# A Mamba, MLP and attention block on one Trainium2 core: v made behind q and k, the first transposed scores ahead of the last score unit, the attention's residual rows ahead of its last division

## The reference, cut to what matters

```
x1 = _ln(x) * (scale1 + 1.0) + shift1
qkv = (x1 @ mat_qkv_w.T + qkv_bias).reshape(B, L, 3, H, hd)      # qkv_bias: q_bias, zeros, v_bias
q, k, v = [jnp.transpose(qkv[:, :, i], (0, 2, 1, 3)) for i in range(3)]
q = _l2norm(q) * sm                                              # 16 heads of 16 channels
k = _l2norm(k)
probs = jax.nn.softmax(jnp.einsum('bhqd,bhkd->bhqk', q, k), axis=-1)
o = jnp.einsum('bhqk,bhkd->bhqd', probs, v)
attn_out = o @ proj_w.T + proj_b
x = x + attn_out * gamma1
...                                                              # a second layer norm and an MLP of width 1024
```

## Time and profile before

| | |
|---|---|
| median of 3 runs | 3436.22 us (3434.76 to 3437.71) |
| the profiled execution | 3437.39 us |
| its span | 3435.6 us, 60533 instructions |
| PE busy | 3272.0 us (95%) |
| DVE busy | 2798.0 us (81%) |
| ACT busy | 2803.2 us (82%) |
| POOL busy | 2501.9 us (73%) |
| TensorE's granted clock over the span | 0.977 of full speed |

### The profile page before, as it was taken

One profiled execution on the slowest core, in us unless ns is written; L12 is line 12 of the kernel. 1 busy time (PEld: TensorE's weight loads), 2 busy tenths in 40 slices (PEclk: granted clock), 3 DMA queues, 4 the chain that ended last, 5 costly groups with the idle time before them and its releaser, 6 DMA issues. The chain is left out here.

```text
span 3435.6 us, 60533 instructions
## 1 busy us (share of the span) xinstructions
PE 3272.0 (95%) x23720; PEld 2705.5 (79%) x23720; DVE 2798.0 (81%) x3009; ACT 2803.2 (82%) x4960; POOL 2501.9 (73%) x1104
## 2 busy tenths in 40 slices
PE   7999999999899999999989999999999999999998
PEld 6889898974488988897368898899637898888744
DVE  2899999976299999996639999999554999999761
ACT  1989999964498999995559999999356999999734
POOL 1899999960098999994029999999204999999700
PEclk9999999998999999999999999999989999999989
DMA  3221211100111121220021222212002221111000
GB/s 131 84 64 56 72 56 64 62 32 13 53 62 64 62 69 52 70 68 25 1 70 57 64 70 64 63 58 68 13 1 78 68 64 68 55 57 56 31 13 7
DMA packets 57088, 187.71 MB, mean 55 GB/s; under 512 B 6626, under 2 KB 12770, under 8 KB 55906
## 3 DMA queue, kind: packets, MB, share of 16 engines
q1 hardware_dynamic: 56802, 183.84, 16.0%
HBM read 180.65 MB, written 3.16 MB: 54 GB/s over the span
## 5 line engine op out<-in xcount | busy, mean ns | idle before, releaser
L543 POOL TENSOR_TENSOR states<-states,c_rows 128x1024 f32<-128x1024 f32 x1020 | 2394.7, 2382 | 499.0 <-DMA c_rows<-c_spill 411.8
L1356 DVE TENSOR_TENSOR_SCAN states<-decay,bank 128x512 f32<-128x512 f32 x2048 | 2350.9, 1203 | 214.8 <-ACT decay L684 143.0
L684 ACT ACTIVATE decay<-dt,a_log 128x512 f32<-128x512 f32 x2048 | 1307.2, 712 | 0.5 <-DVE states L1356 0.5
L937 PE MATMUL bank<-ident,states 128*128 128x128 f32 x8192 | 1237.3, 274 | 18.2 <-POOL states L543 0.3
L926 PE MATMUL bank<-ident,inflow_tok 128*128 128x128 f32 x6144 | 1046.3, 279 | 59.8 <-DVE states L1356 42.9
L678 ACT ACTIVATE inflow_tok<-dtx_tok,b_tok 128x512 f32<-128x512 f32 x1536 | 995.4, 714 | 61.8 <-PE bank L927 58.5
L937 PEld LDWEIGHTS bank<-ident,states 128*128 128x128 f32 x8192 | 955.0, 142 | 50.4 <-POOL states L543 47.9
L926 PEld LDWEIGHTS bank<-ident,inflow_tok 128*128 128x128 f32 x6144 | 707.5, 141 | 241.6 <-issue 128.9
L927 PE MATMUL bank<-b_diag,dtx_tok 128*128 128x128 f32 x4096 | 794.5, 276 | 0.0
L927 PEld LDWEIGHTS bank<-b_diag,dtx_tok 128*128 128x128 f32 x4096 | 621.0, 192 | 0.0
L1444 DVE TENSOR_REDUCE decay<-bank 128x1 f32<-128x512 f32 x256 | 159.7, 684 | 68.0 <-PE bank L1118 67.7
(11 more groups left out here) (152 smaller groups left out, 2039.3 us busy)
## 6 DMA issues: line engine op xcount, KB each, us to landing
c_rows<-c_spill SPq DMA_DIRECT2D x256, 512.0 KB, 3.7
xproj_w<-in_xproj_w SPq DMA_DIRECT2D x32, 320.0 KB, 4.3
in_w<-in_in_w SPq DMA_DIRECT2D x16, 512.0 KB, 4.9
in_w<-in_fc_w SPq DMA_DIRECT2D x8, 512.0 KB, 5.3
xproj_w<-in_w SPq DMA_DIRECT2D x8, 512.0 KB, 5.2
xproj_w<-in_fc_w SPq DMA_DIRECT2D x4, 1024.0 KB, 4.8
y_gated<-in_mod_w SPq DMA_DIRECT2D x1, 2048.0 KB, 7.4
x_ahead<-in_x SPq DMA_DIRECT2D x4, 512.0 KB, 5.6
```

The costliest lines, as they stand in the source:

```text
L543: pool.tensor_tensor(pair, pair, c_row, ALU.mult).then_inc(weighed, 1)
L684: act.activation(decay[:, r % SLOTS * KI + k, :], dt[:, d, k, :], ACT.Exp, scale=a_neg[:, d, k, s:s + 1]).then_inc(decay_ready, 1)
L937: last = pe.matmul(banks[KI + t][:, k * P:(k + 1) * P], states[:, r % SLOTS * KI + k, t * P:(t + 1) * P], ident[:], is_transpose=True, sta ...
L1356: dve.tensor_tensor_scan(states[:, slot, time], decay[:, slot, time], banks[k % INFLOW_BANKS][:, time], 0.0, ALU.mult, ALU.add).then_inc(s ...
```

## The change

It does four things.

- v is made after all four tiles of q and k, in banks 2 and 3 (two tiles to a bank). Its bias is put in the bank by a matmul with one row, ahead of the two of the product, and ACT (instead of DVE) copies it to `v_ones`, two tiles at a time. The five `WARM` matmuls are gone. The wait for v moves from in front of the first score unit to the third and the fourth, whose banks it uses.
- The ring of score banks starts at bank 1 instead of bank 0, and the ring of transposed scores at bank 6 instead of bank 3. So of the score units 31, 32 and 33, the first two wait for lead units 25 and 26 and the third for lead unit 30; before it was 30, 25 and 26.
- In period 0 the third score unit stands behind the four transposed scores.
- Three of the four pairs of `add_rows` for the attention's residual stand ahead of the last transpose of sums (one) and ahead of the last division's result (two); the fourth stands behind the transposes of o.

```diff
-WARM = 5
+V_BANK = 2
...
         def score_bank(u):
-            return banks[u % LEAD_BANKS] if u < LEAD else banks[score_slot(u) % S_BANKS]
+            return banks[u % LEAD_BANKS] if u < LEAD else banks[ring_bank(score_slot(u))]
+
+        def ring_bank(slot):
+
+            return (slot + 1) % S_BANKS
 
         def turn_bank(p):
-            return banks[turn_slot(p) % S_BANKS]
+            return banks[ring_bank(turn_slot(p))]
+
+        def t_bank(v):
+
+            return S_BANKS + (v + T_BANKS - 1) % T_BANKS
...
                 root(TT - 1)
+                act.wait_ge(ones_ready, b + 1)
+                for i in range(2):
+                    act.wait_ge(v_mm, b * TT + 2 * i + 2)
+                    act.activation(v_ones[:, 2 * i:2 * i + 2, :, 0:HD],
+                                   banks[V_BANK + i].rearrange("p (t h e) -> p t h e", t=2, e=HD), ACT.Copy).then_inc(v_ready, 1)
...
-                    act.activation(probs_t[v % len(probs_t)], banks[S_BANKS + v % T_BANKS], ACT.Exp,
+                    act.activation(probs_t[v % len(probs_t)], banks[t_bank(v)], ACT.Exp,
...
                     for kc in range(KD):
-                        pe.matmul(banks[QK_BANK + t % 2], h_t[:, kc, t * P:(t + 1) * P], qkv_w[:, kc, 0:2 * D],
-                                  start=(kc == 0), stop=(kc == KD - 1))
-                    for kc in range(KD):
-                        last = pe.matmul(banks[t][:, 0:D], h_t[:, kc, t * P:(t + 1) * P], qkv_w[:, kc, 2 * D:3 * D], start=(kc == 0), stop=(kc == KD - 1))
-                    last.then_inc(qkv_mm, 1)
+                        last = pe.matmul(banks[QK_BANK + t % 2], h_t[:, kc, t * P:(t + 1) * P], qkv_w[:, kc, 0:2 * D],
+                                         start=(kc == 0), stop=(kc == KD - 1))
+                    last.then_inc(qk_mm, 1)
                     if t == 0:
                         ln_turn(b, 2, 2)
                         ln_turn(b, 2, 3)
-                for w in range(WARM):
-                    pe.matmul(banks[TURN_BANK + 1], ident[:], qkv_w[:, w % KD, 0:2 * D], start=True, stop=True)
+
+                def value_tile(t):
+
+                    to = banks[V_BANK + t // 2][:, t % 2 * D:(t % 2 + 1) * D]
+                    pe.matmul(to, ident[0:1, 0:1].to_broadcast([1, P]), row_b[0:1, V_BIAS, :], start=True, stop=False,
+                              skip_group_check=True)
+                    for kc in range(KD):
+                        last = pe.matmul(to, h_t[:, kc, t * P:(t + 1) * P], qkv_w[:, kc, 2 * D:3 * D], start=False,
+                                         stop=(kc == KD - 1), skip_group_check=True)
+                    last.then_inc(v_mm, 1)
+
+                for t in range(TT):
+                    value_tile(t)
 
...
                 turn_heads(0)
-                pe.wait_ge(v_ready, (b + 1) * TT)
                 pe.wait_ge(q_t_first, b + 1)
...
                     if x < S_BANKS:
-                        pe.wait_ge(neg_ready, b * UNITS + lead_last(x) + 1)
+                        pe.wait_ge(neg_ready, b * UNITS + lead_last(ring_bank(x)) + 1)
...
                     elif u >= LEAD_BANKS:
                         pe.wait_ge(neg_ready, b * UNITS + u - LEAD_BANKS + 1)
+                    elif u in (V_BANK, V_BANK + 1):
+                        pe.wait_ge(v_ready, b * TT // 2 + u - V_BANK + 1)
...
-                    if v < LEAD_BANKS - S_BANKS:
-                        pe.wait_ge(neg_ready, b * UNITS + lead_last(S_BANKS + v) + 1)
+                    if v == 0:
+                        pe.wait_ge(qk_t_ready, (b + 1) * (2 * NG - 1))
                     elif v < T_BANKS:
-                        pe.wait_ge(qk_t_ready, (b + 1) * (2 * NG - 1))
+                        pe.wait_ge(neg_ready, b * UNITS + lead_last(t_bank(v)) + 1)
                     else:
                         pe.wait_ge(probs_t_ready, b * UNITS + v - T_BANKS + 1)
                     a = slice(i * LANE, (i + 1) * LANE)
-                    pe.matmul(banks[S_BANKS + v % T_BANKS], k_t[a, g, kt * P:(kt + 1) * P], q_t[a, g, :], start=True,
+                    pe.matmul(banks[t_bank(v)], k_t[a, g, kt * P:(kt + 1) * P], q_t[a, g, :], start=True,
                               stop=True).then_inc(scores_t_mm, 1)
...
                         scores_t(v)
                         scores(u + 1)
                         scores_t(v + 1)
-                        scores(u + 2)
+                        if j:
+                            scores(u + 2)
                     else:
                         scores_t(v)
                         scores_t(v + 1)
                     scores_t(v + 2)
                     scores_t(v + 3)
+                    if j == 0:
+                        scores(u + 2)
                     if j:
                         weigh(j - 1)
                     if j in TURN_PERIODS:
...
                 weigh(PERIODS - 1)
+                pe.wait_ge(proj_gated, (b + 1) * 3)
+                rows = [t for t in reversed(range(TT)) if t != ring_bank(turn_slot(PERIODS))]
+                pe.wait_ge(neg_ready, (b + 1) * UNITS)
+                add_rows(rows[0], x_mlp, 0)
                 slot_free(turn_slot(PERIODS))
                 turn_lanes(NG - 1, turn_bank(PERIODS))
+                pe.wait_ge(o_ready, (b + 1) * NG - 1)
+                add_rows(rows[1], x_mlp, 0)
+                add_rows(rows[2], x_mlp, 0)
                 pe.wait_ge(o_ready, (b + 1) * NG)
                 for t in range(TT):
                     for f in range(KD):
                         last = pe.transpose(banks[O_BANK + f][:, t * P:(t + 1) * P], o_rows[:, t, f * P:(f + 1) * P], ident[:])
                 last.then_inc(o_turned, 1)
-                pe.wait_ge(proj_gated, (b + 1) * 3)
-                for t in range(TT):
-                    add_rows(t, x_mlp, 0)
+                add_rows(ring_bank(turn_slot(PERIODS)), x_mlp, 0)
                 pe.wait_ge(o_t_ready, (b + 1) * KD)
                 for t in range(TT):
                     residual_tile(t, lambda c, t: o_t[:, c, t * P:(t + 1) * P], lambda c: proj_g[:, c, :], KD)
...
-                dve.wait_ge(ones_ready, b + 1)
...
                 for t in range(TT):
-                    dve.wait_ge(qkv_mm, b * TT + t + 1)
+                    dve.wait_ge(qk_mm, b * TT + t + 1)
                     dve.tensor_tensor(qk[:, t, 0:D], banks[QK_BANK + t % 2][:, 0:D], row_b[:, Q_BIAS, :],
                                       ALU.add).then_inc(q_ready, 1)
-                    dve.tensor_tensor(v_ones[:, t, :, 0:HD], banks[t][:, 0:D].rearrange("p (h e) -> p h e", e=HD),
-                                      row_b[:, V_BIAS, :].rearrange("p (h e) -> p h e", e=HD),
-                                      ALU.add).then_inc(v_ready, 1)
                     if t:
```

More of the change, by code:

```diff
@@ L323, in build @@
         mlp_ready = sem("mlp_ready")
-        qkv_mm = sem("qkv_mm")
+        qk_mm = sem("qk_mm")
+        v_mm = sem("v_mm")
         q_ready = sem("q_ready")
```

## The result

The kernel after takes 3389.24 us (median of 4 runs, 3388.83 to 3391.94) against 3435.52 (3434.76 to 3437.71): a ratio of 0.9866, interval 0.9849 to 0.9883. The span is 3387.6 us, 48.0 less than before. The execution of it that is profiled here, 3437.39 us, is one of the slower ones, so against a typical one the gain is 42 to 44 us.

A forecast was written before the change was run, and what follows sets the result against it. The attention was taken as bound by a chain changing hands between engines, not one engine's work. 2.2 + 2.2 + 1.8 = 6.2 us a sequence, four times 24.8, with the clock 28.4, gave 3408 us; range 3394 to 3427.

The forecast's parts named there:

- unit 31: Sign at the start of the periods: DVE has no wait over 1 us there, where it idled 2.16 us.
- the clock: In the lead, a half-clock stretch may go: 1.2 us in each of three sequences, 3.6 us in all.
- q, k and v: Ahead of the first score: with v behind q and k, the scores' transposes start 2.2 us sooner a sequence.
- The end: From last weighing to projection: residual rows moved into PE's waits let the projection start 1.8 us sooner a sequence.
- an outer bound of 0.9: At the projection: running it at the full clock saves 0.9 us, as in the second sequence; counted only in the upper bound.
- Period 0: At the start of the periods: DVE's wait at score unit 31 goes, 2.2 us a sequence.
- My bounds of 1.7 to 3.4: Start of the periods, up to the first weighing: gain of 1.7 us with the clock down, 3.4 with it up.
- The lead: From the first score on: it moves with its first score; its clock may save up to 2.4 us, or none.
- More arrives: Rival: half-clock stretches of the lead shorten everywhere and the projection runs at full clock; 3395 us, chance 0.10.
- Slower: Rival: granted clock falls to 0.50 at tile 2 of q and k; +4 us a sequence, 3452 us, chance 0.04.
- The first weighing: Sign in the first period: it comes 45 to 48 us after the first q matmul, 51.6 before.

The follow-up runs named there:

- after_no_bias: The kernel after without the four one-row matmuls that add v's bias (its output lacks that bias); 3409.86 us.
- before_all_filled: The kernel before, order unchanged, with unread matmuls in the gaps ahead of the scores, in lead, layer norms, periods and attention's end; 3403.02 us.
- gap_filled: The kernel before with two more unread matmuls in the thin stretch ahead of the first score, its five others kept; 3427.42 us.
- after_both_fillers: The kernel after with unread matmuls behind the lead's units 12 to 30 and in the gaps of the two layer norms; 3372.43 us.

## Why the prediction was wrong

The mechanisms and their places were right, and so were the signs announced for q, k, v, for unit 31 and for the end. What failed is one term, the clock: 3.6 us in all were forecast for it, in the lead, and about 26 were measured. Of the 19.6 us between the 28.4 us of the forecast and the 48.0 of the spans, 10.4 lie in the lead, 5.1 behind the projection, where the forecast had nothing, and 3.6 in period 0; the last 0.5 is the end.

- **q, k and v.** Forecast 2.2 us, measured 2.18. The end of `unit` came 15.13 us after the first q matmul (15.1 forecast) and v's last record started at 14.91, a tie as forecast. A bias matmul costs 0.83 us a tile by the estimate, 0.63 of its own and 0.2 at its neighbour, and `after_no_bias` shows it: 3.3 us for four.
- **The end.** Forecast 1.8, measured 1.93 (7.22 us for 7.4). Behind the projection came another 1.28 us on average, 1.6 in three sequences and 0.25 in the second. I had kept this as an outer bound of 0.9 and put nothing in the sum; the second sequence before, which has the projection at the full clock, already showed 8.74 us against 10.14, 1.40 less.
- **Period 0.** Forecast 2.2, measured 3.10. No wait for DVE at unit 31, as announced, and none for unit 33 either. The 2.2 was DVE's wait in a stretch at half clock: 1.3 of order plus 0.9 of clock. My bounds of 1.7 to 3.4 held it.
- **The lead, the failed step.** "So a half-clock stretch may go, which saves up to 2.4 us [...] I take half, 1.2 us, for three: 3.6 us in all." Measured: 3.50 a sequence, 14.0 in all. Halving was one fault. The larger one was the ceiling: I took the second sequence as the undisturbed lead, and its granted clock is 0.79 in the very row. It is the better of two disturbed ones. The rows held the answer: with levels 1.00 and 0.50, 0.69 means 17.5 of 28.29 us at half clock, 0.79 means 10.9 of 25.88. So 6.7 us at half clock cost 2.41, and the other 10.9 would cost 3.9 more: about 22.0 us at the full clock by estimate, where `before_all_filled` measured 22.46. The ceiling of the gain was 28.29 - 22.46 = 5.8 us in three sequences (0.95 of it in the wait for unit 31) and 3.4 in the second, not 2.4 in three.
- **What each term would have been.** Order 5.4 us a sequence, 21.7 in all; clock 3.5 (lead), 1.8 (period 0) and 1.3 (from the projection), 6.6 a sequence, 26 in all. Forecast: 24.8, with 0.9 of clock a sequence hidden in it, and 3.6.
- **The rivals.** "More arrives", 3395 us at 0.10, names what happened, and was 6 us short by the same ceiling. "Slower" did not come: after v the granted clock stays at 1.00. But `after_no_bias` shows that it was close, in another place than I put it: not between tiles 2 and 3, but behind v. I had weighed "activity releases the throttle" (the Trainium skill, "TensorE: Matmul & The Clock Gate", What's actually happening) only as a threat, the loss of the fillers; `gap_filled` shows the other side of it, that more PE work in a thin stretch makes a later one faster. The first weighing was to come at 45 to 48 us, and 41.4 to 43.1 was outside it on the good side.

What stays open: why the half clock appears at about 28 to 34 us in three sequences of the kernel after and not in the first, where the same instructions run; and why the norms' fillers bring it there in all four. Fillers in the lead remove it, so it can be prevented; no run here explains it.

## What to carry to other kernels

Before costing an edit, read the granted clock of each stretch it touches, and work out from two disturbed windows what the stretch would take at the full clock; the better of two windows is no floor while its clock is under 1.00. An edit that fills PE's time ahead of a dense stretch is worth its own gain plus the clock behind it, and one that thins it (a "free" removal of work off the path) can cost more than it saves. Separate the two by putting unread matmuls into the gaps of the old order: what they win is clock, and the rest is order.

## What the hardware showed that I had not expected

- Four one-row matmuls a sequence taken away, which moved the first score by only 0.22 us, made the kernel 20 us slower: with 1.32 us of PE work in 4.72 ahead of the scores the granted clock fell to 0.50 under them, with 4.16 in 4.94 it did not.
- A stretch in which the profile marks PE busy throughout can hold half clock. The fourth sequence's lead after is 22.89 us with 22.89 busy, at 0.85; its matmuls use 32 rows of the array and come one per DVE reduction of 0.61 us. With 38 more small records in it (101 to 139) it reads 1.00.
- Busy time counts a slower clock as work: by estimate some 20 of the 28.5 us by which PE's busy time fell were not work removed.
- The kernel before shows its sequences in more than one pattern of clock, so that the second took 3.9 us less than its sisters for the same instructions; in `after_both_fillers` all four take 101.46 us.
